# A selective-scan layer with routed experts on one core: the prologue in another order

## The reference

```
xn = layernorm(x)
# sequence branch, D_IN = 1024 channels, N = 16 states per channel, R = 32
proj  = xn @ W_in.T                     # first half: x branch, second half: gate
xb    = silu(causal_conv4(x branch) + conv_b)
ts, B, C = rms(each part of xb @ W_x.T)          # 32 + 16 + 16 rows, called "ssm" below
dt    = softplus(ts @ W_dt.T + b_dt)             # the step sizes
state = state * exp(dt * A) + (dt * xb) * B      # the scan over time, per channel and state
y     = sum_n state * C + xb * D
s     = (y * silu(gate)) @ W_out.T
# expert branch, 8 experts, top 2 per token
logits = xn @ gate_w ; two largest, softmax weights
g     = silu(weighted sum of xn @ expert_w[e] over the two experts)
out   = x + s * g
```

## Time and profile before

| | us |
|---|---|
| median of 3 runs | 1041.59 (1041.16 to 1045.15) |
| the profiled execution | 1042.27 |
| its span in the profile | 1040.4 |
| DVE busy | 982.7 (94%) |
| POOL busy | 905.7 (87%) |
| PE busy | 850.3 (82%) |
| ACT busy | 732.0 (70%) |

### The profile page before, as it was taken

The page is one execution under the profiler, slowest core; times in us unless marked ns, Lnnn a source line. Parts: engine busy times, 40 slices in busy tenths (PEclk is TensorE's granted clock), DMA queues, the critical chain, the costliest instruction groups (busy, mean ns, idle before and its releaser), DMA issues.

```text
span 1040.4 us, 10333 instructions
## 1 busy us (share of the span) xinstructions
PE 850.3 (82%) x2756; PEld 316.3 (30%) x2756; DVE 982.7 (94%) x1027; ACT 732.0 (70%) x1281; POOL 905.7 (87%) x320
## 2 busy tenths in 40 slices
PE   8945469889879998999755859989898999988568
PEld 6321113333323343333211313333332333323123
DVE  6779999999999999999999999999999998999997
ACT  3556767888887667888665566888878776777543
POOL 0626899999889998998799987999988999999996
PEclk9986669999999999999876979999998998999789
DMA  9947578667678666575833742856548565564735
GB/s 332 349 164 274 212 250 312 237 270 265 233 279 299 233 241 209 196 253 188 258 97 126 225 181 101 303 195 217 202 142 291 185 222 209 222 223 152 264 51 151
DMA packets 81978, 229.15 MB, mean 220 GB/s; under 512 B 8833, under 2 KB 10241, under 8 KB 75265
## 3 DMA queue, kind: packets, MB, share of 16 engines
q1 hardware_dynamic: 67712, 197.03, 52.8%
q0 software_dynamic: 6144, 16.78, 6.3%
q10 hardware_dynamic: 8064, 14.68, 3.7%
HBM read 116.00 MB, written 45.35 MB: 155 GB/s over the span
## 4 chain that ended last, share of the span: by engine, by line
DVE 29%; POOL 24%; PE 19%; issue 13%; ACT 13%; DMA 2%; SPq 1%; ACTq 0%; DVEq 0%; POOLq 0%
POOL drive L605 14%; DVE sc_ps L1197 10%; POOL drive L618 6%; DVE drive L1207 5%; DVE drive L1197 5%; ACT sc_ps L818 4%; PE x_ps L1525 4%; PE dt_ps L1453 3%; PE f_ps L1478 3%; PE y_ps L1493 2%; POOL moe L590 2%; ACT L960 2%; DVE x_ps L1126 1%; PE x_ps L1411 1%; ACT L952 1%
## 5 line engine op out<-in xcount | busy, mean ns | idle before, releaser
L605 POOL TENSOR_TENSOR drive<-rep,b_all 128x2048 f32<-128x2048 f32 x127 | 579.5, 4602 | 26.2 <-DMA rep<-dtu 13.8
L818 ACT ACTIVATE sc_ps<-rep,a_neg 128x512 f32<-128x512 f32 x512 | 332.1, 681 | 93.5 <-DVE drive L1207 70.7
L618 POOL TENSOR_TENSOR drive<-drive,c_all 128x1024 f32<-128x1024 f32 x92 | 219.7, 2388 | 16.0 <-ACT state L797 11.9
L1493 PE MATMUL y_ps<-drive,stack 128*32 128x512 f32 x1024 | 149.9, 661 | 94.4 <-DVE drive L1207 61.7
L1197 DVE TENSOR_TENSOR_SCAN sc_ps<-sc_ps,state,drive 128x512 f32<-128x512 f32 x164 | 202.5, 1272 | 5.4 <-ACT sc_ps L818 3.8
L1207 DVE TENSOR_TENSOR drive<-sc_ps,c_all 128x1024 f32<-128x1024 f32 x164 | 199.3, 1215 | 2.8
L1197 DVE TENSOR_TENSOR_SCAN sc_ps<-sc_ps,drive 128x512 f32<-128x512 f32 x164 | 193.4, 1214 | 6.9 <-ACT sc_ps L818 5.2
L1478 PE MATMUL f_ps<-w_ring,xT_slot 128*128 128x512 f32 x368 | 172.3, 612 | 26.4 <-ACT xT_slot L828 26.4
L1453 PE MATMUL dt_ps<-xnT,w_g 128*128 128x512 f32 x232 | 124.4, 686 | 25.6 <-ACT dtu L785 22.4
L1197 DVE TENSOR_TENSOR_SCAN drive<-sc_ps,state,drive 128x512 f32<-128x512 f32 x92 | 113.7, 1267 | 4.0 <-ACT sc_ps L818 4.0
L1197 DVE TENSOR_TENSOR_SCAN drive<-sc_ps,drive 128x512 f32<-128x512 f32 x92 | 109.7, 1209 | 1.1 <-ACT sc_ps L818 0.5
(11 more groups left out here) (189 smaller groups left out, 1058.3 us busy)
## 6 DMA issues: line engine op xcount, KB each, us to landing
rep<-dtu SPq DMA_DIRECT2D x128, 512.0 KB
w_ring<-wring SPq DMA_DIRECT2D x46, 1024.0 KB, 5.0
x_slot<-slot_x SPq DMA_DIRECT2D x46, 256.0 KB, 4.2
slot_rows<-y_slot ACTq DMA_DIRECT2D x46, 256.0 KB
...
```

Source lines behind the costliest of these rows:

```text
L605: pool.tensor_tensor(drive[:, m % RING, :, :], rep[:, n % 2, :, 1, :], b_all[:, q:q + 1, :].broadcast_to([P, NR, TC]), ALU.mult).then_inc( ...
L618: pool.tensor_tensor(drive[:, m % RING, 0:2, :], drive[:, m % RING, 0:2, :], c_all[:, q:q + 1, :].broadcast_to([P, 2, TC]), ALU.mult).then ...
L818: act.activation(sc[:, r, :], rep[:, n % 2, r, 0, :], ACT.Exp, scale=a_neg[:, lo:lo + 1]).then_inc(decay_ok, 1)
L1493: last = pe.matmul(y_ps[CH * r:CH * (r + 1), :], stack[:, :], drive[:, m % RING, r, :], start=False, stop=(m % NQ == NQ - 1))
```

## The change

All of it lies in the prologue and in tile 0 of the loop; the arithmetic is the same.

- SP: `x_w` is loaded in two halves with a semaphore each. The order is half 0, x tiles 4 to 7, the eight constants, half 1, x tiles 8 to 15. The stores to `xn_rows` count in two semaphores, one per batch row; the first spread waits for the first only (and for 8 transposes, not 16), the other wait comes after `take_first`.
- Normalising: DVE takes tiles 11 to 15 (before 12 to 15) with a semaphore of its own, and puts them between its convolutions, without waiting for POOL: tile 11 behind convolution 4, tiles 12 and 13 behind 5, 14 behind 6, 15 behind 7. POOL keeps 4 to 10.
- DVE convolves tile 2 ahead of the last statistics and tile 3 ahead of the roots on which POOL waits.
- PE: all eight `project_x` one behind the other, then all eight `add_ssm`, then one transposed tile (4), the means, transposes 5 to 8, `step_sizes(0)`, transposes 9 to 14, `step_sizes(1)`, transpose 15, the router. Before, transposes 4 to 9 stood among the last `add_ssm`, and `step_sizes(1)` behind the router.
- ACT: five `copy_x` ahead of the second roots, silu in groups; the table load ahead of `rms(0)`; transposed tiles 4 to 7, 11 and 12; the copy of the logits behind the decays of quad 0; the exponential of the weights inside tile 0.
- DVE copies transposed tiles 8, 9, 10, 13, 14 and 15 out (before 7, 8, 9).
- DVE: `rms(0)`, turns 8 to 10, `step_sizes(0)`, turns 13 to 15, all of `step_sizes(1)`, quad 0, then `route_ranks` ahead of quad 1, and `route_rows` and `route_weights` behind quad 1. `count_pairs` on PE is behind `gate_in(0)`.
- POOL waits for `pick_ok` ahead of the drives of quad 3 (whose buffer `beats` uses), no longer ahead of quad 0.

```diff
--- before.py
+++ after.py
@@ -31,8 +31,8 @@
 TILES = NCH * NT
 QUADS = NQ * TILES
 RING = 4
-LAST_NORMS = 12
-VECTOR_TURNS = (7, 8, 9)
+LAST_NORMS = 11
+VECTOR_TURNS = (8, 9, 10, 13, 14, 15)
 WARM = 26
 REP = 16 * NR
 RT = SEQ // P
@@ -323,6 +323,11 @@
         def drives_done(eng, count):
             eng.wait_ge(drive_ok, count)
 
+        def norms_done(eng, count):
+            eng.wait_ge(xn_ok, min(count, LAST_NORMS))
+            if count > LAST_NORMS:
+                eng.wait_ge(xn_dv, count - LAST_NORMS)
+
         def rows_put(eng, b):
             if b == 0:
                 eng.wait_ge(s_scat[2], 16 * 2 * RT)
@@ -338,16 +343,25 @@
         def _(sp):
             for i in range(TT // 2):
                 sp.dma_start(x_in[:, i, :], x_t[i]).then_inc(s_x0[i], 16)
-            sp.dma_start(x_w[:, :, :].rearrange("p t (k m) -> p t k m", k=HK),
-                         wx_in.rearrange("t p k m -> p t k m")).then_inc(s_xw, 16)
+            def load_x_w(k):
+                lo, hi = HK * k, HK * (k + 1)
+                sp.dma_start(x_w[:, lo:hi, :].rearrange("p t (k m) -> p t k m", k=HK),
+                             wx_in[lo:hi].rearrange("t p k m -> p t k m")).then_inc(s_xw[k], 16)
+
+            def load_x(g):
+                for i in range(TT):
+                    sp.dma_start(x_in[:, g * TT + i, :], x_t[g * TT + i]).then_inc(s_x[g], 16)
+
+            load_x_w(0)
+            load_x(1)
             for dst, src in ((a_neg[:, :], a_log), (w_ssm[:, :, :], wxp), (w_gate, gate_w),
                              (cw[:, :], conv_w), (cb[:, :], conv_b), (dsk[:, :], d_skip),
                              (mean_w[0:SSM, :], means),
                              (consts[:, :], route_consts)):
                 sp.dma_start(dst, src).then_inc(s_const, 16)
-            for g in range(1, NCH):
-                for i in range(TT):
-                    sp.dma_start(x_in[:, g * TT + i, :], x_t[g * TT + i]).then_inc(s_x[g], 16)
+            load_x_w(1)
+            for g in range(2, NCH):
+                load_x(g)
 
             def load_w_g(n):
                 if n:
@@ -369,8 +383,8 @@
             sp.wait_ge(zero_ok, 1)
             clear_slots(0, 0, SLOTS)
             for k in range(16):
-                sp.wait_ge(xn_ok, k + 1)
-                sp.dma_start(xn_rows[P * k:P * (k + 1), :], x_in[:, k, :]).then_inc(s_xn, 16)
+                norms_done(sp, k + 1)
+                sp.dma_start(xn_rows[P * k:P * (k + 1), :], x_in[:, k, :]).then_inc(s_xn[k // RT], 16)
 
             def stage_xnT():
                 for c in range(2, NCH):
@@ -470,14 +484,16 @@
 
             store_rows(0)
             spread_b(0, 0)
-            sp.wait_ge(s_xn, 16 * 16)
-            sp.wait_ge(tr_mm, 16)
+            sp.wait_ge(s_xn[0], 16 * RT)
+            sp.wait_ge(tr_mm, RT)
             spread(0)
             spread_c(0, 0)
             for q in range(1, NQ):
                 spread_b(0, q)
                 spread_c(0, q)
             take_first()
+            sp.wait_ge(s_xn[1], 16 * RT)
+            sp.wait_ge(tr_mm, 2 * RT)
             stage_xnT()
 
             for n in range(TILES):
@@ -641,7 +657,6 @@
                                    ALU.subtract, ALU.mult).then_inc(xn_ok, 1)
 
             pool.wait_ge(conv_ok, NT)
-            pool.wait_ge(pick_ok, 1)
             pool.wait_ge(s_b[0], 16)
             for h in range(2):
                 pool.wait_ge(s_rep[0][h], REP // 2)
@@ -659,6 +674,8 @@
                 if gathers:
                     gather_first(c - 1)
                 put_rows(*PUTS.get((n, 0), (0, 0)))
+                if n == 0:
+                    pool.wait_ge(pick_ok, 1)
                 drives(NQ * n + 3)
                 low_products(NQ * n + 1)
                 if gathers:
@@ -739,22 +756,22 @@
             copy_transposed(range(TT))
             act.wait_ge(s_const, 16 * 8)
             act.activation(a_neg[:, :], a_neg[:, :], ACT.Exp).then_inc(a_exp, 1)
-            for t in range(4):
+            for t in range(5):
                 copy_x(t)
             act.wait_ge(ln_v, 2)
             link(act.activation(nl[:, TT:], nv[:, TT:], ACT.Ln))
             act.activation(nr[:, TT:], nl[:, TT:], ACT.Exp, scale=-0.5).then_inc(ln_r, 1)
 
             act.preload_act_table_set(SILU)
-            silu_x(0)
-            silu_x(1)
-            for t in range(4, NT):
-                copy_x(t)
-                silu_x(t - 2)
-            silu_x(NT - 2)
-            copy_transposed(range(TT, 6))
-            silu_x(NT - 1)
-            copy_transposed(range(6, 7))
+            copy_x(5)
+            for t in range(3):
+                silu_x(t)
+            copy_x(6)
+            for t in range(3, 5):
+                silu_x(t)
+            copy_x(7)
+            for t in range(5, NT):
+                silu_x(t)
 
             def exponent(k):
                 act.wait_ge(dt_mm, k + 1)
@@ -900,20 +917,21 @@
                 link(act.activation(t_w[0:SSM, :], mean_bank(c)[0:SSM, :], ACT.Ln, bias=eps[0:SSM, 0:1]))
                 act.activation(t_w[0:SSM, :], t_w[0:SSM, :], ACT.Exp, scale=-0.5).then_inc(ssm_r, 1)
 
+            act.preload_act_table_set(LNEXP)
             rms(0)
-            act.preload_act_table_set(LNEXP)
+            copy_transposed(range(TT, TT + 1))
             rms_root(0)
-            copy_transposed(range(10, 16))
+            copy_transposed(range(TT + 1, 8))
             softplus(0)
-            act.wait_ge(lgT_mm, 1)
-            act.copy(logit_T[:, :], f_ps[:, :]).then_inc(lgT_ok, 1)
+            copy_transposed(range(11, 13))
             keep_dt(0)
             softplus(1)
             act.wait_ge(a_ok, 1)
+            turns_done(act, 2 * RT)
             decays(0, 0)
             decays(0, 1)
-            act.wait_ge(lg_d, 1)
-            act.activation(weight, weight, ACT.Exp).then_inc(lg_e, 1)
+            act.wait_ge(lgT_mm, 1)
+            act.copy(logit_T[:, :], f_ps[:, :]).then_inc(lgT_ok, 1)
 
             for n in range(TILES):
                 c, t = divmod(n, NT)
@@ -942,6 +960,9 @@
                 if early is not None:
                     copy_x(NT * (c + 1) + early)
                 decays(m + 1, 1)
+                if n == 0:
+                    act.wait_ge(lg_d, 1)
+                    act.activation(weight, weight, ACT.Exp).then_inc(lg_e, 1)
                 copy_slot_T(b, first_slot)
                 if n in SILU_SOON:
                     act.preload_act_table_set(SILU)
@@ -1028,7 +1049,7 @@
             def normalise(tiles):
                 for k in tiles:
                     dve.tensor_scalar(x_in[:, k, :], x_in[:, k, :], mv[:, k, 0:1], nr[:, k:k + 1],
-                                      ALU.subtract, ALU.mult).then_inc(xn_ok, 1)
+                                      ALU.subtract, ALU.mult).then_inc(xn_ok if k < LAST_NORMS else xn_dv, 1)
 
             def roots(count, lo, hi):
                 dve.wait_ge(ln_r, count)
@@ -1131,24 +1152,31 @@
                 for k in range(1, K):
                     tap(j, k)
 
+            def turn(tiles):
+                for k in tiles:
+                    dve.wait_ge(tr_mm, k + 1)
+                    dve.tensor_copy(*turned(k)).then_inc(tr_dv, 1)
+
             spreads(1)
             dve.wait_ge(a_exp, 1)
             dve.tensor_scalar(a_neg[:, :], a_neg[:, :], -1.0, None, ALU.mult).then_inc(a_ok, 1)
             convolve(0)
             spreads(2)
             convolve(1)
+            convolve(2)
             spreads(3)
             variances(TT, NCH * TT)
-            convolve(2)
+            convolve(3)
             roots(2, TT, NCH * TT)
             dve.sem_inc(rs_ok, 1)
-            for t in range(3, NT):
-                convolve(t)
-            dve.wait_ge(xn_ok, LAST_NORMS)
-            normalise(range(LAST_NORMS, NCH * TT))
-            for k in VECTOR_TURNS:
-                dve.wait_ge(tr_mm, k + 1)
-                dve.tensor_copy(*turned(k)).then_inc(tr_dv, 1)
+            convolve(4)
+            normalise(range(LAST_NORMS, LAST_NORMS + 1))
+            convolve(5)
+            normalise(range(LAST_NORMS + 1, LAST_NORMS + 3))
+            convolve(6)
+            normalise(range(LAST_NORMS + 3, LAST_NORMS + 4))
+            convolve(7)
+            normalise(range(LAST_NORMS + 4, NCH * TT))
 
             def times_x(k):
                 c, t = divmod(k, NT)
@@ -1243,20 +1271,16 @@
                                          op0=ALU.mult, op1=ALU.mult).then_inc(dtin_ok, 1)
 
             rms(0)
+            turn(range(8, 11))
             step_sizes(0)
-            route_ranks()
-            larger_part(1)
-            less_rounding(1)
-            plus_log(1)
-            route_rows()
-            times_x(1)
+            turn(range(13, 16))
+            step_sizes(1)
             scan(0, 0)
             scan(0, 1)
             low_product(0)
             scan(0, 2)
             scan(0, 3)
             products(0, 1)
-            route_weights()
             for n in range(TILES):
```

(32 more changed lines are left out.)

6 lines of the change are left out of this document (3 added, 3 removed).

## The result

The changed kernel takes 1047.07 us (median of 10 runs, 1046.07 to 1049.18); the kernel before took 1041.52 beside it on the same chip. The ratio is 1.0051 (95% interval 1.0043 to 1.0059): slower by 5.5 us or 0.5%, inside the range, at about half the forecast's +10.4. The profiled execution of after took 1047.23 with a span of 1045.0 (before 1042.27 and 1040.4).

What follows compares the result with a forecast made beforehand. DVE bounds the kernel, through its arrival at quad 4. Without contention +1.1 us, norms held +6.1 and `beats` held +3.2 sum to +10.4, a median of 1052.0 us; range 1040.5 to 1056.

Steps and rivals of the forecast that it cites:

- The bound: Whole kernel: DVE is almost full, so a shift of its arrival at quad 4 (112.70) reaches the end one for one.
- The rival in which POOL sets the pace: Tiles 1 to 8: POOL sets the pace, the 8.4 us gain stays, time 1033.2; chance 0.10.
- The earlier ssm: Prologue up to the ssm: unbroken projections end the additions at 48.0 instead of 52.13, a gain of 4.1 us.
- The landing: First spread: second half lands 7.4 us behind its issue, at 68.9, so quad 0 starts at 69.6, gain 8.4.
- The norms, +6.1: DVE's norms among convolutions each wait for POOL's instruction under way, making the ssm 6.1 us later; lower bound 0.
- `beats`, +3.2: Ranks behind quad 0: this comparison with both inputs in SBUF waits 3.2 us for POOL's drive of quad 2.
- The routing, +10.05: Behind quad 0: DVE gets back the ranks, 6.05 us, and the rows, 4.0, that stood ahead of it.
- The wait inside quad 0: DVE's quad 0 in tile 0: no added wait was forecast; it was to end 7.0 us behind its start.
- beats alone: Rival: only the ranks' comparison waits for POOL, not the norms: +4.3 us, 1045.9; chance 0.07.
- the case without any hold: Rival: POOL holds neither DVE's norms nor the ranks' comparison: +1.1 us, 1042.7; chance 0.21.
- The likeliest case: Full forecast: POOL holds both the norms and the ranks' comparison, +10.4 us, 1052.0; chance 0.47.

Runs made afterwards that it cites:

- experiment 11: Changed kernel with routing back in its old place, POOL's old `pick_ok` wait, transpose 13 earlier and ACT's scaled rows later: 1037.30 us, ratio 0.9958 against the kernel before.
- experiments 8 and 9: Changed kernel repeated unchanged: 1047.48 us, ratio 1.0056; beside it, with POOL's wait for the ranks ahead of quad 2's drives instead of quad 3's: 1045.07, ratio 1.0031.
- Experiment 4: Separate kernel with only DVE and POOL instructions of these shapes, alone and side by side: eight DVE norms took 5.44 us beside POOL's norms instead of 3.8.
- experiment 5: Changed kernel with DVE's five norms in one piece behind the last convolution instead of between convolutions: 1046.77 us, ratio 1.004 against the kernel before.
- Experiment 3: Kernel before with the routing alone moved (ranks ahead of quad 1, rows and weights behind it): 1051.45 us, ratio 1.0084.

## Why the prediction was right in its sign and wrong in its size

- **The bound.** Right for this change: DVE's arrival at quad 4 sets the end. The shift there (5.36) is the shift at the ninth tile (5.45) and of the medians (5.5). The rival in which POOL sets the pace is out: DVE waits for a drive only inside quad 0 (0.51 us), and the drive of quad 4 is done 20 us before DVE gets there (97.84 and 118.06). In experiment 11 the end gained less than quad 4, so "one for one" is no rule.
- **The earlier ssm.** Right: the square moved by 4.6 us for the 4.1 of the sum. DVE kept up as worked out (the instruction behind convolution 4 began at 36.05, the time in the text).
- **The landing.** The 7.4 us of the earlier trace rows were taken over, and it took 9.2. Of these 1.8 us, 0.7 were made up by an earlier issue (60.81 for 61.5), so quad 0 came 1.1 late. The cause is not shown (experiments 8 and 9).
- **The norms, +6.1.** This is the step that failed. It took the wait of an addition beside POOL's two-input product for a norm beside POOL's one-input norm. Experiment 4 shows that the first pair waits to the end and the second doesn't, and experiment 5 that the place of the norms costs nothing that shows. In after the norms lost 0.9 us in sum, which a wait for ACT took up. The lower bound of that term was right. By the Trainium skill, "SBUF — State Buffer", section "Who interferes with whom", whichever of GpSimd and a DVE instruction in a two-port mode issues first has the shared pair of ports for its whole instruction. The rows of experiment 4 agree for GpSimd's `tensor_tensor` (a norm took 4.17 us, 3.6 more than alone, beside 4.50) and not for its `tensor_scalar` (8 norms 1.6 us later in all beside 8.57); the measurement decides.
- **`beats`, +3.2.** Right in kind, 2.34 in size: it came at 78.86, 1.8 us later than worked out (1.1 by the landing, 0.6 by the wait inside quad 0), and POOL's second product ended only 1.0 later (81.34 for 80.3).
- **The routing, +10.05.** Right: ranks 6.07 and rows 4.14 came back behind quad 0. Experiment 3 shows them with the rest left out: quad 4 8.6 us later for 4.0 gained at quad 0.
- **The wait inside quad 0, +0.6.** Missed: POOL makes the second half of its drive (2.36) from the landing on, and DVE now arrives with it instead of 5 us behind it.
- **Which case it was.** Without the norms' term, the sum is that of the rival "beats alone", +4.3, which had a chance of 0.07; the landing (+1.1) and quad 0 (+0.6), less what `beats` was held for less (-0.85), bring it to about 5.2. That the measured time still lies inside the range is owed to its width, which had been drawn to reach the case without any hold. The likeliest case joined two holds as one mechanism, although only one had a row of its own kind.
